# An LSTM scan over 1024 steps: i, g and f through one ScalarE operation, the f matmuls behind i and g, the loop body turned by a step, the layer's weights prepared late

## What is computed

```
def step(carry, xw_t):                  # xW = x @ Wx + b, Wx: [256, 1024]
    prev_h, prev_c = carry
    a = xw_t + prev_h @ Wh              # Wh: [256, 1024]
    i = sigmoid(a[:, :H]); f = sigmoid(a[:, H:2*H]); o = sigmoid(a[:, 2*H:3*H]); g = tanh(a[:, 3*H:])
    next_c = f * prev_c + i * g
    next_h = o * tanh(next_c)
    return (next_h, next_c), next_h
x = x + scan(step, (h0, 0), x)
# then a modulated linear layer, with ys = h0 / sqrt(256)
d = rsqrt(einsum('bi,io->bo', ys * ys, weight * weight) + EPS)
x = x + einsum('bsi,io->bso', x * ys[:, None, :], weight) * d[:, None, :]
```

## Time and profile before

| | us |
|---|---|
| median of 3 runs | 2107.36 (2089.85 to 2110.37) |
| the profiled execution | 2090.74 |
| its span, first to last instruction | 2088.9 |
| TensorE matmuls busy | 1787.2 (86%) |
| TensorE weight loads busy | 1630.4 (78%) |
| VectorE busy | 1320.4 (63%) |
| ScalarE busy | 1058.6 (51%) |
| GpSimd busy | 259.2 (12%) |

### The profile page before, as it was taken

One profiled execution on the slowest core, in us unless ns is written; L12 is line 12 of the kernel. 1 busy time (PEld: TensorE's weight loads), 2 busy tenths in 40 slices (PEclk: granted clock), 3 DMA queues, 4 the chain that ended last, 5 costly groups with the idle time before them and its releaser, 6 DMA issues.

```text
span 2088.9 us, 286931 instructions
## 1 busy us (share of the span) xinstructions
PE 1787.2 (86%) x127160; PEld 1630.4 (78%) x127160; DVE 1320.4 (63%) x12572; ACT 1058.6 (51%) x8196; POOL 259.2 (12%) x1287
## 2 busy tenths in 40 slices
PE   5888888888888888888888888888888888888888
PEld 5787777777777777777788777777778777777776
DVE  3666666666666666666666666666666666666665
ACT  3555555555555555555555555555555555555553
POOL 0111111111111111111111111111111111111110
PEclk9999999999999999999998999999999999999999
DMA  2000000000000000000000000000000000000001
GB/s 87 0 0 0 0 0 0 0 0 0 0 0 0 0 0 0 0 0 0 0 0 0 0 0 0 0 0 0 0 0 0 0 0 0 0 0 0 0 0 40
DMA packets 4570, 6.65 MB, mean 3 GB/s; under 512 B 1234, under 2 KB 3028, under 8 KB 4564
## 3 DMA queue, kind: packets, MB, share of 16 engines
q1 hardware_dynamic: 3872, 5.51, 0.8%
q10 hardware_dynamic: 692, 1.05, 0.1%
HBM read 4.46 MB, written 2.10 MB: 3 GB/s over the span
## 4 chain that ended last, share of the span: by engine, by line
PE 55%; DVE 21%; ACT 17%; issue 6%; DMA 0%; SPq 0%; POOL 0%; DVEq 0%; POOLq 0%
PE pA L193 28%; PE pS L200 15%; DVE junk L329 9%; ACT tanhc L165 8%; PE pA L177 6%; DVE hst L338 6%; ACT gates L156 5%; PE pA L171 5%; DVE pT L325 5%; ACT gates L154 5%; DVE gates L329 1%; PE pA L270 1%; DMA w_sb<-in_w_dram 0%; SPq L104 0%; PE pT L183 0%
## 5 line engine op out<-in xcount | busy, mean ns | idle before, releaser
L200 PE MATMUL pS<-hst,wh_sb 128*32 128x2 f32 x65536 | 1052.0, 176 | 2.4 <-issue 2.3
L193 PE MATMUL pA<-wh_sb,hst 128*2 128x64 f32 (+1 forms) x32768 | 810.3, 225 | 267.7 <-DVE hst L338 255.9
L200 PEld LDWEIGHTS pS<-hst,wh_sb 128*32 128x32 f32 x65536 | 1021.8, 111 | 2.6 <-issue 2.5
L325 DVE STREAM_TRANSPOSE pT<-pA 128x64 f32<-128x64 f32 x2048 | 481.6, 263 | 582.7 <-PE pA L193 582.1
L193 PEld LDWEIGHTS pA<-wh_sb,hst 128*2 128x2 f32 (+1 forms) x32768 | 549.7, 88 | 374.8 <-DVE hst L338 373.9
L154 ACT ACTIVATE gates<-pS 128x2 f32<-128x2 f32 x2048 | 353.5, 173 | 918.8 <-PE pS L200 918.7
L329 DVE CUSTOM_DVE_ANT_0 junk<-gates 128x4 f32<-128x4 f32 x4096 | 465.6, 159 | 39.4
L165 ACT ACTIVATE tanhc<-gates 128x2 f32<-128x2 f32 x2048 | 410.8, 204 | 54.8
L133 POOL TENSOR_TENSOR xh<-xh,hst 128x4 f32 x1024 | 206.9, 202 | 1725.0 <-DVE hst L338 1725.0
L338 DVE TENSOR_TENSOR hst<-tanhc,gates 128x2 f32<-128x2 f32 x2048 | 328.4, 160 | 111.1 <-ACT tanhc L165 3.4
L156 ACT ACTIVATE gates<-pT 128x4 f32<-128x4 f32 x2048 | 356.9, 177 | 18.6
(11 more groups left out here) (31 smaller groups left out, 37.1 us busy)
## 6 DMA issues: line engine op xcount, KB each, us to landing
outT_dram<-ores SPq DMA_DIRECT2D x8, 256.0 KB, 2.5
xh<-in_xT_dram SPq DMA_DIRECT2D x6, 320.0 KB, 7.8
wx_sb<-in_Wx_dram SPq DMA_DIRECT2D x1, 1024.0 KB, 5.1
wh_sb<-in_Wh_dram ACTq DMA_DIRECT2D x1, 1024.0 KB, 7.6
w_sb<-in_w_dram SPq DMA_DIRECT2D x1, 256.0 KB, 8.4
xh<-in_xT_dram SPq DMA_DIRECT2D x2, 64.0 KB, 7.8
bias_sb<-in_bT_dram ACTq DMA_DIRECT2D x2, 1.0 KB
condT<-in_condT_dram ACTq DMA_DIRECT2D x1, 2.0 KB, 5.3
```

The lines of the kernel that those rows point to most:

```text
L193: last = pe.matmul(pA[j][c * Q:c * Q + M, 0:PAIR * Q].rearrange("p (g u) -> p g u", u=Q), hst[:, k, lo:lo + M], two(wh_sb[:, k, :], c, j, ...
L200: last = pe.matmul(pS[c * Q:(c + 1) * Q, n, B * t:B * (t + 1)], tile(wh_sb[:, k, :], c, j, g), hst[:, k, h_slot(t):h_slot(t) + B], start=F ...
L325: dve.transpose(pT[j][:, 0:PAIR * Q], pA[j][:, 0:PAIR * Q]).then_inc(turned_ready[j], 1)
```

## The change

- PSUM: pT and the f sums of a half become neighbouring banks of one tile `pB`. One activation (L185 of the new file) reads i and g from the one and f from the other, eight values of which two are not used. Its semaphore counts both the transpose and the f matmuls. `gates` is laid out anew, o goes to its own tile `ogate`.
- TensorE's order in a step: all of `turned`, then f, then o, instead of f in between.
- The body runs t=1, 2, 3, 0. `sum_x` comes in 4 and 4 sets behind t=1 and t=2. The fills stay behind t=3 and wait for the second activation (`gates_ready[1]`) instead of the second transpose. Behind t=0 TensorE waits for GpSimd's addition and does one `filler`, a matmul of 128 columns of zeros. VectorE no longer waits for GpSimd.
- `carry_x` is split: f ahead of the writes of h in t=3, o behind them.
- 32 fillers run ahead of the loop. w and most of x are loaded after the first steps. GpSimd squares and modulates w in the loop. The sums and the square root come behind the loop.

```diff
-    CELL = 16
-    AT_F, AT_O, AT_G, AT_HALF, AT_C = 3, 6, 9, 10, 11
+    CELL = 8
+    AT_I, AT_F, AT_G, AT_HALF, AT_C = 0, 1, 2, 4, 5
+    WARM = 32
...
-        pT = [ctx.enter_context(nc.psum_tensor(f"pT{j}", [P, 512], F32)) for j in range(K)]
-        pS = ctx.enter_context(nc.psum_tensor("pS", [P, PAIR * K, 512], F32))
-
-        pD, pX, pO = pA[0], pT[0][:, AT_X:AT_X + PAIR * K * ROWS], pA
+        pB = ctx.enter_context(nc.psum_tensor("pB", [P, K, PAIR, 512], F32))
+        pS = ctx.enter_context(nc.psum_tensor("pS", [P, K, 512], F32))
+
+        pT = [pB[:, j, 0, :] for j in range(K)]
+        sums = [pB[:, j, 1, :] for j in range(K)] + [pS[:, j, :] for j in range(K)]
+        pD, pX, pO = pS[:, 0, :], pT[0][:, AT_X:AT_X + PAIR * K * ROWS], pA
...
+            sp.wait_ge(h_ready[0], 2 * T)
...
+            def bodies(lo, hi, aside=None):
+                with pool.Fori(lo, hi) as it:
+                    for s in range(T):
+                        for j in range(K):
+                            pool.wait_ge(h_ready[j], it * T + (s + 2))
+                        at = h_slot((s + 2) % T)
+                        now = xh[:, :, :, bass.ds(it * T + (s + 1), 1)]
+                        pool.tensor_tensor(now, now, hst[:, :, at:at + B].unsqueeze(3), ALU.add).then_inc(xh_ready, 1)
+                    pool.wait_ge(filled, it + 2)
+                    spread(bass.ds(it * T + 2 * T, T))
+                    if aside is not None:
+                        aside()
...
+            EARLY = XCUT[1] // T - 3
+            bodies(0, EARLY)
...
+            for k in range(K):
+                bodies(EARLY + k, EARLY + k + 1, lambda: squares(k))
+            for n in range(B * K):
+                bodies(EARLY + K + n, EARLY + K + n + 1, lambda: modulated(n // K, n % K))
+            bodies(EARLY + K + B * K, NBODY)
...
+            act.wait_ge(zeros_ready, 1)
+            act.activation(warmed[:, :], zeros[:, 0:1], ACT.Sigmoid)
+
+            with act.Fori(0, NBODY) as it:
+                for s in range(T):
+                    t = (s + 1) % T
+                    cols = slice(B * t, B * (t + 1))
+                    for j in range(K):
+                        act.wait_ge(turned_and_fsum_ready[j], it * (2 * T) + 2 * (s + 1))
+                        act.activation(gates[:, j, :, 0:2 * PAIR].rearrange("p b (q a) -> p a q b", a=PAIR),
+                                       pB[:, j, :, 0:PAIR * Q].rearrange("p a (q r) -> p a q r", q=PAIR)[:, :, :, cols],
+                                       ACT.Sigmoid).then_inc(gates_ready[j], 1)
+                    for j in range(K):
+                        act.wait_ge(osum_ready[j], it * T + (s + 1))
+                        act.activation(ogate[:, j, :], sums[K + j][:, cols], ACT.Sigmoid)
+                        act.wait_ge(cell_ready[j], it * T + (s + 1))
+                        act.activation(tanhc[:, j, :], gates[:, j, :, AT_C], ACT.Tanh, scale=2.0).then_inc(tanh_ready[j], 1)
+
             act.wait_ge(demod_added, 1)
             act.activation(demod[:, :, :], demod[:, :, :], ACT.Sqrt).then_inc(demod_rooted, 1)
...
+            def filler(start):
+                pe.matmul(pA[0][0:Q, P:2 * P], picks[:, :], zeros[:, :], start=start, stop=True, skip_group_check=True)
...
+            for _ in range(WARM):
+                filler(True)
...
             with pe.Fori(0, NBODY) as it:
-                for t in range(T):
-                    pe.wait_ge(h_ready[0], it * T + (t + 1))
+                for s in range(T):
+                    t = (s + 1) % T
+                    pe.wait_ge(h_ready[0], it * T + (s + 1))
                     turned(t, 0, 0)
                     turned(t, 1, 0)
+
+                    pe.wait_ge(h_ready[1], it * T + (s + 1))
+                    turned(t, 0, 1).then_inc(sums_ready[0], 1)
+                    turned(t, 1, 1).then_inc(sums_ready[1], 1)
                     if t == 0:
-                        pe.wait_ge(x_carried, it + 1)
-                    still(t, F_, 0, 0, range(0, G // 2))
-
-                    pe.wait_ge(h_ready[1], it * T + (t + 1))
-                    turned(t, 0, 1).then_inc(sums_ready[0], 1)
-                    still(t, F_, 0, 0, range(G // 2, G))
-                    still(t, F_, 0, 1).then_inc(fsum_ready[0], 1)
-                    turned(t, 1, 1).then_inc(sums_ready[1], 1)
-                    still(t, F_, 1, 0)
-                    still(t, F_, 1, 1).then_inc(fsum_ready[1], 1)
+                        pe.wait_ge(x_carried[0], it + 2)
+                    for j in range(K):
+                        still(t, F_, j, 0)
+                        still(t, F_, j, 1).then_inc(turned_and_fsum_ready[j], 1)
+                    if t == 0:
+                        pe.wait_ge(x_carried[1], it + 2)
                     for j in range(K):
                         still(t, O_, j, 0)
                         still(t, O_, j, 1).then_inc(osum_ready[j], 1)
 
-                    if t < T - 1:
-                        if t == 0:
+                    if s < PAIR:
+                        if s == 0:
                             pe.wait_ge(xp_ready, it + 2)
-                        pe.wait_ge(gates_ready[0], it * T + (t + 1))
-                        for n, k in XSHARE[t]:
+                        pe.wait_ge(gates_ready[0], it * T + (s + 1))
+                        for n, k in XSUMS[s * len(XSUMS) // PAIR:(s + 1) * len(XSUMS) // PAIR]:
                             last = sum_x(n, k)
-                        if t == T - 2:
+                        if s == PAIR - 1:
                             last.then_inc(x_summed, 1)
-                    else:
-                        pe.wait_ge(turned_ready[1], it * T + T)
+                    elif t == T - 1:
+                        pe.wait_ge(gates_ready[1], it * T + (s + 1))
                         for j in range(K):
                             fill_bias(j)
                         for j in range(K):
                             for k in range(K):
                                 last = fill_x(j, k)
                         last.then_inc(filled, 1)
-
+                    else:
+                        pe.wait_ge(xh_ready, it * T + (2 * T - 1))
+                        pe.wait_ge(gates_ready[0], it * T + (s + 1))
+                        filler(False)
+
+            pe.wait_ge(squares_ready, K)
+            pe.wait_ge(x_carried[1], NBODY + 1)
+            pe.wait_ge(h_ready[0], SEQ + 1)
+            for o in range(K):
+                for k in range(K):
+                    last = pe.matmul(pD[:, o * B:(o + 1) * B], wsq[:, k, o * P:(o + 1) * P], ysq[:, k, :],
+                                     start=(k == 0), stop=(k == K - 1))
+            last.then_inc(demod_summed, 1)
...
+            def carry_x(n):
+                at = n * K * ROWS
+                into = pS if n else pB[:, :, 1, :]
+                dve.tensor_tensor(into[:, :, 0:ROWS], pX[:, at:at + K * ROWS].rearrange("p (j r) -> p j r", r=ROWS),
+                                  bias_col[:, n * K:(n + 1) * K].unsqueeze(2).broadcast_to([P, K, ROWS]),
+                                  ALU.add).then_inc(x_carried[n], 1)
...
+            with dve.Fori(0, NBODY) as it:
+                for s in range(T):
+                    t = (s + 1) % T
+                    for j in range(K):
+                        dve.wait_ge(sums_ready[j], it * T + (s + 1))
+                        dve.transpose(pT[j][:, 0:PAIR * Q], pA[j][:, 0:PAIR * Q]).then_inc(turned_and_fsum_ready[j], 1)
+                    for j in range(K):
+                        dve.wait_ge(gates_ready[j], it * T + (s + 1))
+                        for b in range(B):
+                            cell = dve.tensor_tensor_reduce(
+                                out=junk[:, j, b, :], in0=gates[:, j, b, AT_I:AT_F + 1].unsqueeze(2).broadcast_to([P, 2, 2]),
+                                in1=gates[:, j, b, AT_G:AT_G + 6].rearrange("p (a c) -> p a c", a=2)[:, :, ::2],
+                                scale=1.0, scalar=0.0, op0=ALU.mult, op1=ALU.add,
+                                accum_out=gates[:, j, b, AT_C:AT_C + 1])
+                        cell.then_inc(cell_ready[j], 1)
+                    if t == T - 1:
+                        dve.wait_ge(x_summed, it + 2)
+                        carry_x(0)
+                    at = h_slot((t + 1) % T)
+                    for j in range(K):
+                        dve.wait_ge(tanh_ready[j], it * T + (s + 1))
+                        dve.tensor_tensor(hst[:, j, at:at + B], tanhc[:, j, :], ogate[:, j, :], ALU.mult).then_inc(h_ready[j], 1)
+                    if t == T - 1:
+                        carry_x(1)
+
```

138 lines of the change are left out of this document (44 added, 94 removed).

## The result

The changed kernel takes 2193.36 us (median of four runs, 2187.21 to 2199.69) against 2108.86 us for the kernel before on the same chip: a ratio of 1.042, interval 1.035 to 1.049. It is slower by 4%, where 1996 us had been forecast. The profiled execution took 2187.21 us.

The account below looks back on a forecast made before the run. Bound: one long circle of dependences through h, with no engine full. 2090.74 - 84.5 (body) - 7.2 (start) - 3 (warm) + 0.4 (end) - 2 (shorter loop) = 1994.4; plus 2 for spread, 1996 us; range 1948 to 2042.

Parts of the forecast that it names:

- Shorter loop at the same share of low clock: -2: Whole loop: the share of time at low clock stays as before, so a shorter loop saves 2 us more.
- Rival (b): TensorE's clock in the loop falls about twice as often, through the thinner t=0: 2042 us, chance 0.13.
- (a): TensorE's clock in the loop falls less often, as denser steps or the filler keep 2.4 GHz: 1949 us, chance 0.13.
- Rival (e): The two-bank activation costs its upper bound, +0.17 us, on the chain of all 1024 steps: 2160 us, slower, chance 0.06.
- Half 1's loads earlier: TensorE, each step: with f's matmuls behind, turned loads of h half 1 start 0.06 us earlier, at most 0.07.
- Joined activation +0.01: ScalarE, each step: one activation for i, g, f takes 0.01 us longer, at most 0.17.
- This gives nothing: ScalarE, each step: two of eight operations disappear but lay inside a wait, so no time is saved.
- F in time: Joined activation: f is good for 0.79 us, the transpose's path needs it at 0.89, so 0.10 in hand, no cost.
- t=3 ended by the fills, 1.91: Step t=3: TensorE's fills, waiting for the second activation, decide its length of 1.91 us; the h side needs 1.88.
- Body 7.46: Loop body: three steps of 1.85 and one of 1.91 us, 0.33 less than 7.79, times 256: -84.5 us.
- Start: Ahead of the loop: first step at 13.6 instead of 20.77 us, -7.2; bounds -3.2 and -9.
- Warm first bodies, -3: First two bodies: the 32 fillers ahead of the loop may warm the clock, saving 3 us (0 to 4).

Follow-up runs that it names:

- b_order: The kernel before with only the f matmuls moved behind both groups of turned ones, no fillers: 2192.5 us, ratio 1.045.
- the short pad: The changed kernel plus one VectorE memset of 128x128 that nobody reads, once a body in t=1: 2087.15 us, ratio 0.989.
- a_fill_order_old: The changed kernel with fillers (one behind t=1 and t=2, three behind t=0) and f's matmuls back between the turned groups: 2040.95 us, ratio 0.972.
- a_fill_apart: The changed kernel with fillers (one behind t=1 and t=2, three behind t=0) and separate activations for f and i, g: 1996.95 us, ratio 0.952.
- a_fill_no_warm: The changed kernel with one filler behind t=1 and t=2, three behind t=0, without the 32 ahead of the loop: 1962.9 us, ratio 0.930.

## Why the prediction was wrong

**The step that failed** is the last term of the sum, "Shorter loop at the same share of low clock: -2". It carried the share of low clock over from the kernel before, as if the clock didn't depend on what was being changed. It measured +184. With it the sum is 1994.4 + 2 + 183.6 = 2180.0. The small terms below bring +5.9 (body), -1.7 (start), -0.1 (end) and +3 (the warm bodies are in the 184 already): 2187.1, and the profiled execution took 2187.2.

**Rival (b) had the right sign and missed the size.** Its price per fall came out: "about 1 us lost in each" measured 239.3 / 216 = 1.1. Its count did not. It took "about twice as often", from one second set of falls, where there were 4.5 times as many (216 against 48). Nothing in the rows bounded that count, so the upper end of the range was a guess. The rival's reason, the thin t=0, isn't needed: b_order has a thick t=0 and spends 726 us at 1.2 GHz, nearly as long as the change. And (a)'s reason, denser steps keep the clock, pointed the wrong way: the full-clock body of the change has TensorE busy 6.72 of 7.48 us, 90%, against 6.69 of 7.79, 86%, before, and falls more.

The price per fall holds only where the low stretches are as long as here. In b_order 104 of them cost 191 us, 1.8 each, as they last 6.83 us. A price per us at 1.2 GHz carries over better: 0.33 us before, 0.31 in the change, 0.26 in b_order and 0.29 with the short pad, each worked out from the loop's time above 256 full-clock bodies and the loop's time at 1.2 GHz.

The prediction also misread a row. It has the clock fall while TensorE was busy 3.18 of 3.40 us, but that row is the stretch behind the fall, which came at 1037.17. The 3.41 us ahead of it read:

```profile
1033.76:1037.17 3.41, 2.70 (x223) 2.45 (x210) 2.40 (x23) 2.09 (x16) 0.40 (x2) 1.00 0.00 0
```

TensorE was busy 2.70 us there, and 2.98 of 3.42 us ahead of the change's fall at 1008.12. So the change fell behind a denser stretch than the kernel before did. That idle time alone doesn't foretell a fall is still so, but by other rows than the prediction gave: the change fell behind 0.44 us idle of 3.42, while the full-clock body of the earlier trace rows had 1.10 idle of 7.79 and 207 bodies of that kernel kept the clock.

**Rival (e)**, the only one on the slow side, gave 2160 and a slower kernel, by a mechanism that didn't come about: the two-bank activation takes 0.184 us. Its time is nearer than the forecast by luck.

**Point by point at full clock:**
- Half 1's loads earlier, transposes 0.17 apart, first transpose 0.59 after the loads: measured 0.174 and 0.587. Steps t=1, t=2 take 1.845 and 1.846, forecast 1.85. a_fill_order_old confirms the cause.
- Joined activation +0.01: 0.184 us, against 0.173 and 0.177 for the two before. Right in duration; the +0.007 over the longer one lies between the prediction's 0.01 and the 0.003 that it worked out beside it. "This gives nothing" for the removed operations was wrong about the new order (a_fill_apart: 36 us); the sum came out right because it started from the old chain, in which the i, g activation did not queue behind f.
- F in time: right. The first activation starts at 0.886, forecast 0.89, ended by the transpose. At 1.2 GHz f is the later one, 335 times: the cover that the prediction called the thinnest of the design is gone there.
- t=3 ended by the fills, 1.91: measured 1.898. t=0, forecast 1.85, takes 1.894: its loads follow the fills without a gap and take 0.50 us instead of 0.45, a price of standing directly behind the fills that the prediction did not pass on.
- Body 7.46: measured 7.483, so -78.6 instead of -84.5.
- Start: first step at 11.89, forecast 13.6. The 64 loads took 8.24 us, inside "7 to 14", and ended at 10.17, where the prediction had them end at 12. So -8.9 for -7.2.
- Warm first bodies, -3: without the 32 fillers the kernel is at most 2 us slower (a_fill_no_warm).
- End: +0.3 by the spans for +0.4. The table load (1.28) was hidden, as forecast: the square root begins at 2168.10, when the sums are there (VectorE's operation on them ends at 2168.06). That is 1.44 us behind the end of the last tanh at 2166.66, so no switch of 2.66 us, the figure that the prediction cites, shows in this trace.

```profile
1.93 8.24 PEld L233 LDWEIGHTS pA<-zeros,picks 128*32 128x32 f32 x64
11.89 0.45 PEld L221 LDWEIGHTS pA<-wh_sb,hst 128*4 128x4 f32 x32 [0.38 <-issue]
2166.68 1.28 ACT L195 ACT_TABLE_LOAD   x1
2166.84 1.02 PE L305 MATMUL pS<-ysq,wsq 128*128 128x2 f32 x8 [0.34 <-DVE hst L376]
2167.70 0.30 PEld L314 LDWEIGHTS pA<-xh,wmod 128*128 128x128 f32 x2
```

With the clock held, the forecast's own terms are borne out: a_fill_one_each, the change plus two fillers a body, takes 1955.86, and rival (a), "the clock falls less often", had said 1949.

In the loop rows above TensorE's loads never wait more than 0.52 us, and its clock falls 216 times. The Trainium skill (TensorE: Matmul & The Clock Gate, "Part 1: The HAM clock gate") sets the level by how busy the array has been, and puts the drop down to an idle array or to frequent short idles between groups of matmuls. The trace agrees with the second of these in kind, as there is no long idle, but the page has no number that tells these two bodies apart. The rows decide: TensorE was busy 2.98 of 3.42 us and lost its clock.

## What to carry to other kernels

Where the granted clock is not at 1.0 before a change, the clock is a term of the sum with a sign of its own: price the time at 1.2 GHz from the rows, ask what the change does to the places where TensorE does least, and leave the upper bound open until that is answered. A shorter chain can cost the clock and be slower as a whole; so compare variants at equal clock first, with a few fillers in both, before judging an edit. Spread the fillers: one small one in each of the three steps that end in a wait of TensorE, two a body more than the change had, was worth 237 us here, while four in one place were in the way.

And an operation that lies inside a wait is free only in the order in which it was measured; after a reordering, ask again who is last.
